# First graph layer: the halves of the features are transposed by the DMA queue into two buffers, and their products with weights come one tile later

## What is computed

```python
output = jnp.matmul(adj / adj_scaling_factor, support_q / support_delta)
...
h = jnp.maximum(_layernorm(x, axis=-1), 0.0)
x = x + _L0_gnn_ref(h, adj, ...)
h = jnp.maximum(_layernorm(x, axis=-1), 0.0)
x = x + _L1_gnn_ref(h, adj, ...)
...
# in _L1_gnn_ref, X = h
for s in range(STEPS):
    A = _adj_from_feats(Xa, W1, W2, W3)   # Q = Xa @ W1, K = Xa @ W3, logits = Q @ W2 @ K.T, top-p softmax
    Xf = R @ Xf
    Xa = A @ Xa
    Z = Z + (Xf @ U1s[s] + Xa @ U2s[s])
```

## Time and profile before

| | |
|---|---|
| median of three runs | 1202.13 us (1200.91 to 1208.22) |
| profiled execution, its time | 1202.94 us |
| profiled execution, its span | 1201.2 us |
| busy, share of the span | PE 91%, DVE 82%, ACT 40%, POOL 24% |
| first layer's tiles 1 to 15 | about 90 to 301 us |
| DMA in the whole span | 171.68 MB, mean 143 GB/s |
| instructions of PE | 5402 |

### The profile page before, as it was taken

The page is one execution under the profiler, slowest core; times in us unless marked ns, Lnnn a source line. Parts: engine busy times, 40 slices in busy tenths (PEclk is TensorE's granted clock), DMA queues, the critical chain, the costliest instruction groups (busy, mean ns, idle before and its releaser), DMA issues.

```text
span 1201.2 us, 16645 instructions
## 1 busy us (share of the span) xinstructions
PE 1097.6 (91%) x5402; PEld 513.7 (43%) x5402; DVE 989.4 (82%) x2144; ACT 483.9 (40%) x920; POOL 286.8 (24%) x255
## 2 busy tenths in 40 slices
PE   0478999999899969999999998989899999999987
PEld 0234454455434434444444444434344444444433
DVE  7877777776389999889999800889999999999997
ACT  1764444443743213453532223874003364351061
POOL 6124333333132311211121210131111111112143
PEclk9898999999999989999999998999899999999999
DMA  7054565553243453163164084023667467576667
GB/s 263 26 192 163 182 211 192 201 200 144 73 141 109 147 131 80 45 149 71 45 151 93 22 175 140 36 80 122 223 208 166 92 186 140 176 195 151 236 143 217
DMA packets 190708, 171.68 MB, mean 143 GB/s; under 512 B 144736, under 2 KB 144736, under 8 KB 186528
## 3 DMA queue, kind: packets, MB, share of 16 engines
q1 hardware_dynamic: 190624, 170.71, 49.5%
HBM read 87.84 MB, written 49.28 MB: 114 GB/s over the span
## 4 chain that ended last, share of the span: by engine, by line
DVE 32%; PE 30%; issue 18%; POOL 7%; ACT 6%; DMA 5%; SPq 1%; POOLq 1%; DVEq 0%; ACTq 0%
PE AB L987 5%; PE RB L987 5%; DVE WS L1605 4%; DVE cand L1837 4%; PE UB L816 4%; DVE WS L1834 3%; PE XB L816 3%; PE AB L989 3%; DVE E L1850 3%; PE RB L989 2%; DMA turns<-E 2%; DVE rows L1685 2%; DVE WS L1842 2%; DVE E L1572 2%; DMA AD<-xu_d 2%
## 5 line engine op out<-in xcount | busy, mean ns | idle before, releaser
L1685 DVE TENSOR_REDUCE rows<-E 128x1 f32<-128x2048 f32 x32 | 73.0, 2281 | 86.0 <-ACT E L1221 85.8
L682 POOL TENSOR_TENSOR RT<-RT,AD 128x512 f32<-128x512 f32 x32 | 55.7, 1739 | 256.9 <-ACT RT L1281 256.8
L1605 DVE SCALAR_TENSOR_TENSOR WS<-E,rows 128x2048 bf16<-128x2048 f32 x43 | 110.6, 2613 | 0.4
L1837 DVE MAX8 cand<-WS 128x8 f32<-128x128 f32 x512 | 102.1, 278 | 1.1
L1842 DVE SCALAR_TENSOR_TENSOR WS<-E,rows 128x2048 f32<-128x2048 f32 x32 | 79.4, 2482 | 0.8
L696 POOL TENSOR_TENSOR XX<-WF,XX 128x512 f16<-128x512 f32 x16 | 26.4, 1651 | 222.8 <-ACT XX L1306 222.8
L1850 DVE SCALAR_TENSOR_TENSOR E<-WS,E 128x2048 f16<-128x2048 f32 x32 | 77.1, 2410 | 2.2 <-issue 1.1
L1834 DVE SCALAR_TENSOR_TENSOR WS<-E,rows 128x2048 f32<-128x2048 f32 x32 | 77.3, 2415 | 1.1
L987 PE MATMUL RB<-XR,turns 128*128 128x512 f16 x256 | 62.1, 387 | 11.3 <-DMA turns<-E 11.3
L1258 ACT ACTIVATE E<-E,nmx 128x2048 f32<-128x2048 f32 x32 | 63.7, 1992 | 5.7 <-DVE nmx L1686 5.7
L987 PE MATMUL AB<-VR,turns 128*128 128x512 f16 x256 | 61.4, 383 | 4.6 <-DMA turns<-E 4.6
(11 more groups left out here) (343 smaller groups left out, 2194.5 us busy)
## 6 DMA issues: line engine op xcount, KB each, us to landing
turns<-adj_parts SPq DMA_DIRECT2D x48, 512.0 KB, 4.0
E<-adjT SPq DMA_DIRECT2D x16, 1024.0 KB, 7.6
adj_parts<-turns SPq DMA_DIRECT2D x16, 1024.0 KB, 5.2
AH<-adj_parts SPq DMA_DIRECT2D x16, 512.0 KB, 4.3
z_d<-UO SPq DMA_DIRECT2D x28, 256.0 KB, 2.3
XR<-x SPq DMA_DIRECT2D x4, 1024.0 KB, 11.8
WS<-U SPq DMA_DIRECT2D x4, 1024.0 KB, 5.3
x_d<-WF SPq DMA_DIRECT2D x16, 256.0 KB, 2.1
```

Source lines behind the costliest of these rows:

```text
L1605: return v.scalar_tensor_tensor(junk[t % 2], e, g4[:, k, t:t + 1], e, op, ALU.mult, accum_out=g4[:, F_, t:t + 1])
L1685: ct(v.tensor_reduce(row(A2)[:, t:t + 1], E[:, slot, :], AX.X, ALU.max))
L1837: i = v.max(cand[:, t, 8 * c:8 * c + 8], WS[:, c * PART:(c + 1) * PART])
```

## The change

The transposes and ScalarE's copy are taken out. SP issues a DMA transpose `x0_turn(t)` from XR to one of two buffers, XT and a part of E that is free in this stage. TensorE's products of a tile come one tile later than before, behind layer t those of tile t-2, and so do the readers of them on ScalarE and GpSimd and the store of UO. The last two tiles' products stand behind the last layer product. Counts of a few semaphores follow (`s_xT`, `s_xTc` start at the second layer now).

```diff
+        x0_turned = (XT, E[:, 7, 0:2 * KC * P // 2].bitcast(F16).rearrange("p (h k c) -> p h k c", h=2, k=KC))
...
+            def x0_turn(t):
+                sp.wait_ge(s_xh, t + 1)
+                sp.wait_ge(s_xl, t + 1 + OPEN)
+                if t < 2:
+                    sp.wait_ge(s_mm1, T + OPEN)
+                else:
+                    sp.wait_ge(s_pk, t - 1)
+                sp.dma_start_transpose(x0_turned[t % 2].rearrange("p h k c -> p (h k) c"),
+                                       XR[:, t, :, :].rearrange("p h d -> p (h d)")).then_inc(s_x0T[t % 2], 16)
...
                 l0_stores(t)
+                x0_turn(t)
                 at_out(t + 1, odd)
-                adj_in(t + 3)
+                if t + 3 < T:
+                    adj_in(t + 3)
                 diag_out(t)
-                post0_stores(t - 1)
+                if t >= 2:
+                    post0_stores(t - 2)
...
             l0_stores(0)
+            x0_turn(0)
             at_out(1, 1)
             adj_in(3)
             diag_out(0)
             u_in(3)
-            for t in range(1, T - 3):
+            for t in range(1, T - 1):
                 l0_tile(t, (t + 1) % 2)
-            for t in range(T - 3, T - 1):
-                l0_stores(t)
-                at_out(t + 1, (t + 1) % 2)
-                diag_out(t)
-                post0_stores(t - 1)
...
+            x0_turn(T - 1)
+            post0_stores(T - 3)
...
+            def l0_tile(t):
+                l0_head(t)
+                v_lo(t - 2, of(VR, t - 2))
+                pk_lo(t - 2, 0, t - 2, s_vl, t - 1)
...
+            l0_head(1)
+            l0_tile(2)
             u_lo(3)
-            with pool.Fori(2, T) as t:
+            with pool.Fori(3, T) as t:
                 l0_tile(t)
+            v_lo(T - 2, of(VR, T - 2))
+            pk_lo(T - 2, 0, T - 2, s_vl, T - 1)
...
                 for j in range(T):
-                    if j == T // 4 and n is not None:
-                        x_halves_turned(n)
...
-            def x_halves_turned(n):
-
-                pe.wait_ge(s_pkc, n + OPEN)
-                pe.wait_ge(s_xh, n + 1)
-                pe.wait_ge(s_xl, n + 1 + OPEN)
-                for h in range(2):
-                    for k in range(KC):
-                        c = h * KC + k
-                        i = tr(XB[:, :].bitcast(F16)[:, c * P:(c + 1) * P],
-                               XR[:, bass.ds(n, 1), h, k * P:(k + 1) * P].rearrange("p o d -> p (o d)"), ident[:, :])
-                i.then_inc(s_xT, 1)
...
+            def post0(n, odd, last=False):
+
+                halves = halves_of_turned(x0_turned[odd])
+                pe.wait_ge(s_x0T[odd], 8 * n - 8 * odd + 16)
+                if last:
+                    pe.wait_ge(s_pkc, n + OPEN)
+                    pk_product(n, XB, halves)
                 pe.wait_ge(s_ue, n + OPEN)
...
+                three(UB[:, :], *halves, lambda k: U10p[:, k, 0, :], lambda k: U10p[:, k, 1, :]).then_inc(s_u, 1)
...
+                three(RB[:, :], *halves, lambda k: U11p[:, k, 0, :], lambda k: U11p[:, k, 1, :]).then_inc(s_v, 1)
+                if not last:
+                    pe.wait_ge(s_wpk, 4)
+                    pe.wait_ge(s_pkc, n + OPEN)
+                    pk_product(n, XB, halves)
...
+            layer0(1, 1)
...
-            with pe.Fori(1, T - 1, 2) as odd:
-                layer0(odd, 1)
-                layer0(odd + 1, 0)
-            layer0(T - 1, 1)
-            x_halves_turned(T - 1)
-            post0_last(T - 1)
+            with pe.Fori(2, T, 2) as even:
+                layer0(even, 0)
+                post0(even - 2, 0)
+                layer0(even + 1, 1)
+                post0(even - 1, 1)
+            post0(T - 2, 0)
+            post0(T - 1, 1, True)
...
-            def xT_halves(n):
-                act.wait_ge(s_xT, n + 1 + OPEN)
-                a(XT[:, :, :, :].rearrange("p h k c -> p (h k c)"), XB[:, :].bitcast(F16), ACT.Copy).then_inc(s_xTc, 1)
-
...
-                if not last:
-                    x_hi(t + 1)
+                if x is not None:
+                    x_hi(x)
...
-            def l0_tile(t):
+            def l0_head(t):
                 turn_free(t + 1)
                 adj_hi(t + 1)
-                xT_halves(t - 1)
-                post0(t - 1)
...
             x_hi(0)
-            l0_tile(1)
+            l0_head(1)
+            x_hi(1)
+            l0_head(2)
+            post0(0, 2)
             u_hi(3)
-            with act.Fori(2, T - 1) as t:
-                l0_tile(t)
-            xT_halves(T - 2)
+            with act.Fori(3, T - 1) as t:
+                l0_head(t)
+                post0(t - 2, t)
+            post0(T - 3, T - 1)
             post0(T - 2)
-            xT_halves(T - 1)
-            post0(T - 1, True)
+            post0(T - 1, last=True)
```

More of the change, by code:

```diff
@@ L243, in build @@
         s_part = sem("s_part")
+        s_x0T = [sem(f"s_x0T{odd}") for odd in range(2)]
         s_sqd = sem("s_sqd")
@@ L848, in x_turned @@
                 if n - T > POSTPONED:
-                    pe.wait_ge(s_xTc, n)
+                    pe.wait_ge(s_xTc, n - T)
                 pe.wait_ge(s_xf, n + 1)
@@ L855, in x_rest, with halves_of_turned, pk_product @@
                 less(XB, x_turned_of(n)[:, 0, :, :].rearrange("p k c -> p (k c)"), minus).then_inc(s_xTs, 1)
+            def halves_of_turned(u):
+                return [lambda k, h=h: u[:, h, k, :] for h in range(2)]
             def halves_turned(n):
-                return [lambda k, h=h: x_turned_of(n)[:, h, k, :] for h in range(2)]
-            def pk_product(n, bank):
-                hi, lo = halves_turned(n)
+                return halves_of_turned(x_turned_of(n))
+            def pk_product(n, bank, halves=None):
+                hi, lo = halves or halves_turned(n)
                 three(bank[:, 0:P], lambda k: WPK[:, k, 0, :], lambda k: WPK[:, k, 1, :], hi, lo).then_inc(s_pk, 1)
-            def post0(n):
-                pe.wait_ge(s_xTc, n + 1)
+            def post0(n, odd, last=False):
[4 more added lines that the diff above has]
+                    pk_product(n, XB, halves)
                 pe.wait_ge(s_ue, n + OPEN)
-                three(UB[:, :], xh, xl, lambda k: U10p[:, k, 0, :], lambda k: U10p[:, k, 1, :]).then_inc(s_u, 1)
+                three(UB[:, :], *halves, lambda k: U10p[:, k, 0, :], lambda k: U10p[:, k, 1, :]).then_inc(s_u, 1)
                 pe.wait_ge(s_ve, n + OPEN)
-                three(RB[:, :], xh, xl, lambda k: U11p[:, k, 0, :], lambda k: U11p[:, k, 1, :]).then_inc(s_v, 1)
-                pe.wait_ge(s_wpk, 4)
-                pk_product(n, XB)
-            def post0_last(n):
-                pe.wait_ge(s_xTc, n + 1)
-                pk_product(n, XB)
-                pe.wait_ge(s_ue, n + OPEN)
-                three(UB[:, :], xh, xl, lambda k: U10p[:, k, 0, :], lambda k: U10p[:, k, 1, :]).then_inc(s_u, 1)
-                pe.wait_ge(s_ve, n + OPEN)
-                three(RB[:, :], xh, xl, lambda k: U11p[:, k, 0, :], lambda k: U11p[:, k, 1, :]).then_inc(s_v, 1)
+                three(RB[:, :], *halves, lambda k: U11p[:, k, 0, :], lambda k: U11p[:, k, 1, :]).then_inc(s_v, 1)
[3 more added lines that the diff above has]
+                    pk_product(n, XB, halves)
             pe.wait_ge(s_sup, NG)
@@ L886, in _, with layer0 @@
             adj_product_lo(0, 0)
+            def layer0(t, h):
+                adj_product_hi(t, h)
+                adj_product_lo(t, h)
+            layer0(1, 1)
             pe.wait_ge(s_upart_h, 2)
             pe.wait_ge(s_upart_l, 2)
-            def layer0(t, h):
-                adj_product_hi(t, h)
-                adj_product_lo(t, h, t - 1)
-                post0(t - 1)
-            with pe.Fori(1, T - 1, 2) as odd:
-                layer0(odd, 1)
-                layer0(odd + 1, 0)
-            layer0(T - 1, 1)
-            x_halves_turned(T - 1)
-            post0_last(T - 1)
+            with pe.Fori(2, T, 2) as even:
[5 more added lines that the diff above has]
+            post0(T - 1, 1, True)
             def logits_chunk(s, gq, t, c):
@@ L999, in u_product @@
                 mm(UB[:, :], id_sw[:, :], XR[:, t, 1, :], start=False, stop=False)
[L1000 removed]
+                pe.wait_ge(s_xTc, t + 1)
                 hi, lo = halves_turned(n)
@@ L1013, in p_and_k @@
                     pe.wait_ge(s_pkc, t + T + OPEN)
-                    pe.wait_ge(s_xTc, t + T + 1)
+                    pe.wait_ge(s_xTc, t + 1)
                 pk_product(t + T, UB)
@@ L1090, in postponed @@
                 pe.wait_ge(s_pkc, 2 * T + OPEN)
-                pe.wait_ge(s_xTc, 2 * T)
+                pe.wait_ge(s_xTc, T)
                 for t in range(POSTPONED, T):
@@ L1178, in v_hi, with post0 @@
                 a(VR[:, bass.ds(t, 1), 0, :].rearrange("p o d -> p (o d)"), RT[:, :], ACT.Copy).then_inc(s_vh, 1)
-            def post0(t, last=False):
+            def post0(t, x=None, last=False):
                 if last:
```

14 lines of the change are left out of this document (4 added, 10 removed).

## The result

The changed kernel takes 1258.49 us (median of 4 runs, 1257.89 to 1259.97) against 1204.86 us before (median of 4, 1200.91 to 1208.22): ratio 1.0448, 95% interval 1.0407 to 1.0489. The profiled execution of after took 1258.02 us with a span of 1256.2, 55.0 more than before.

What follows compares the result with a forecast made beforehand. The prediction took the DMA queue's chain to the diagonal store's landing, 14.00 us a tile, as the bound. Its terms 7.4 + 38 + 0.1 - 2.5 + 7.0 gave +50 us, a median of 1252.5 us, range 1240 to 1269.

Steps and rivals of the forecast that it cites:

- second chain: First-layer tile: ScalarE's casts and adj_lo, about 13.5 us, shorter than the queue's 14.00 by about 0.5 us.
- What the removal is worth: TensorE loses 1.0 us of transposes a tile: nothing counted in the loop, -2.5 us from XF(14) to XF(15).
- The stall on SP: First-layer loop: the transpose waits for x_lo and delays at_out and diag_out; a tile grows from 14.00 to 17.8 us.
- middle stage: Tiles 3 to 13 of the first layer: ten tiles, each growing from 14.00 to 17.8 us, +38 us.
- 0 more, my value: First-layer loop: the transpose's data time lies wholly under SP's issue and adds nothing to a tile.
- The second rival: First-layer loop: the transpose's data time comes on top, 12 x 1.3 = 16 us more, 1268 us; chance 0.17.
- low bound: First-layer loop: queue neighbours further apart, the landing may shrink by 0.6 us a tile; with no clock loss 1243.5 us.
- The start: First layer up to XF(3): later diagonal stores and a displaced u_hi(3) put XF(3) at 142.9 instead of 135.52, +7.4 us.
- The tail: XF(15) to first logits product: UO(13)'s store lands late, two tiles of products open, lowered clock; 18.1 us, +7.0.
- The first: First-layer loop: the stall on SP is covered, needing a landing within 3.7 us; about 1200 us, chance 0.05.
- The third: First-layer loop: the diagonal's landing shrinks half-way, to 5.5 us; 12 x -2 = -24, 1228 us; chance 0.08.
- The clock loss: TensorE at half clock behind gaps: 1.7 us each, costing nothing in the loop and 1.7 us in the tail.

Runs made afterwards that it cites:

- e1: Changed kernel with SP issuing the DMA transpose behind the diagonal store instead of ahead of the adjacency store; 1206.76 us, ratio 1.0034 to the kernel before.
- e5: Kernel before with the 64 KB diagonal store issued ahead of the two 1 MB transfers; 1200.73 us in one run.
- e6: Changed kernel with diagonal store first, transpose last and the second layer's loads late; 1200.66 us, ratio 0.9981 to the kernel before.
- e2: Changed kernel without the DMA transposes' transfer, SP's wait kept; only its first layer is read, 16.33 us a tile (whole 7601.62 us, computing with meaningless numbers).
- e4: Changed kernel with the store of UO for tile 13 put ahead of the last transpose at SP's end; 1258.50 us in one run.
- e10: e6 with ScalarE's cast of the next adjacency tile put between v_hi and pk; 1188.68 us, ratio 0.9881 to the kernel before.
- e9: e1 with the second layer's loads behind the stores of UO(13) and UO(14), and UO(13)'s store ahead of the last transpose; 1207.08 us in one run.
- e7: e6 with ScalarE's cast of the next adjacency tile put directly behind x_hi; 1197.92 us, ratio 0.9944 to the kernel before.

## Why the prediction was right

**What bounds the kernel.** Right: e1 and e5 show it from two sides. The queue's order alone moves the tile between 18.28 and 14.09, and the diagonal store's place alone between 14.00 and 13.69. The second chain was put at 13.5 us and takes 13.69.

**What the removal is worth.** Right: nothing in the loop (before and e1 differ by 0.09 us a tile, e5 and e6 not at all), and 3.2 us at the last layer tile, where 2.5 were expected: TensorE began layer 15 3.14 us ahead of XF(14), 0.6 earlier than forecast.

**The stall on SP.** The mechanism was right in each step: x_lo, then the transpose, at_out, diag_out, landing, 5.30 us to XF. The issues came at +2.68, +4.05 and +5.14 where +2.65, +4.0 and +4.95 were forecast. The size was off in two terms, each by 0.2 us: diag_out goes at +5.14 for +4.95, and it lands 7.80 us later for 7.58. This makes 18.24 instead of 17.8 us, with the means 18.28, and ten tiles make the 4.8 us by which the middle stage, and nearly the whole sum, is short. The prediction had put the transpose's data at "0 more, my value" beside a landing of 7.58. The landing grew by 0.22 us over that of before, the difference of two effects: with the wait alone it is 0.21 shorter (e2), and the transfer adds 0.43 to that. The second rival, which put all 1.3 us on top, had the right sign and a third of the effect; the low bound's 0.6 us less was three times too large.

**The start.** +6.67 for +7.4: XF(2) came at 122.79 for 123.4, since diag_out(1) landed after 7.10 us instead of 7.58, and the displaced u_hi cost what was counted. The prediction's own terms for XF(3) add up to 142.7 and not 142.9, and 50 us on the median of 1202.13 are 1252.1 and not 1252.5; neither slip matters.

**The tail.** +7.65 for +7.0, for the reason that was given: ScalarE waits until the store of UO(13) has landed, and that is set by the 1.5 MB ahead of it. UO(14) came 8.47 us after XF(15) for 7.5 (the loads were to go out 0.7 us ahead of XF(15) and went out with it), so the products of tile 15 began at 11.57 for 10.5; at full clock they take 5.85 for 5.9, and the clock cost 1.3 for 1.7. e4's narrower theory, that the issue behind the transpose counts, is the one that fell. What the prediction did not see is that its wait was worth only 2.47 us: the two tiles of products in a row hold the tail at 14.95 without it.

**The whole.** The median is 6.0 us above the 1252.5, inside the range. Of this 4.4 us are missing in the sum of the stages, mostly the loop; the other stages were off by at most 0.7 us each, the start too long and the tail too short, and these two cancel.

**The rivals.** The first (the stall is covered) is out: the diagonal landed after 7.8 us, not under 3.7. The third (the landing shrinks to 5.5) is out by the same number; the second is answered above.

**What was not foreseen.** ScalarE waits 97.9 us in all for the store of UO, which SP issues behind diag_out and which now lands late (229.1 in the tile that starts with XF at 216). It costs nothing in the loop, since x_hi, the next in ScalarE's program, waits for XF 4.8 us longer anyway; the largest wait in the list is one of no worth. The clock loss was forecast for every gap and for 1.7 us, from one row of before that the earlier trace rows does not show:

```profile
112.42 4.45 PE L816 MATMUL UB<-E,XX 128*128 128x512 f16 x12 [2.81 <-ACT XX L1155]
```

It was there behind all but one of the 13 gaps ahead of hi products in after, with 1.3 to 2.8 us more for the sixteen products (next section). It cost nothing in the loop, as forecast, and 1.3 us in the tail.

## What to carry to other kernels

A DMA issue that has to wait for data is more than one transfer added to the queue: it is a barrier in the program of the engine that issues it. Before putting one in, list what stands behind it, and look for the small transfer among that which somebody waits for; put the waiting one last and the small one first. And an engine relieved of work pays only when no other chain is as long: here three had to be shortened together (queue, casts, TensorE) before removing 1 us of transposes from a tile gave 1 us (e5 to e10, 13.69 to 12.74).

## What the runs showed of the hardware

- A DMA transpose of 256 KB held SP's program for 1.26 us as the tile's first large issue (after) and mostly for 2.4 to 2.6 us behind at_out, adj_in and diag_out (e1). In e6 and e10, behind the same three with diag_out first, it held it for 1.5 to 2.1 us; why less was not tested. The plain transfer issued right behind it took 0.52 instead of 0.34 to 0.37 us for its issue. A 64 KB store behind it landed 0.43 us later than in e2, where it was left out (means of ten tiles).
- What a gap costs TensorE can't be read from its length. In after the sixteen hi products took 5.30 us behind a gap of 2.78 us, 6.38 behind one of 3.76 us, but 3.61 behind one of 3.72 us:

```profile
157.03 5.30 PE L818 MATMUL AB<-E,turns 128*128 128x512 f16 x16 [2.78 <-DVE E L1564]
...
175.53 6.38 PE L818 MATMUL AB<-E,turns 128*128 128x512 f16 x16 [3.76 <-DVE E L1564]
...
230.71 3.61 PE L818 MATMUL AB<-E,turns 128*128 128x512 f16 x16 [3.72 <-DVE E L1564]
```

  Windows of after (stretch, us, busy us of PE, PEld, DVE, ACT, POOL, granted clock, DMA share, GB/s) show 1.00 behind that one and 0.50, which is 1.2 GHz, behind a gap of 5.19 us:

```profile
230.70:234.20 3.50, 3.49 (x17) 1.60 (x18) 2.63 (x6) 0.00 (x0) 1.78 (x2) 1.00 0.00 0
...
248.90:252.50 3.60, 3.55 (x9) 1.34 (x10) 2.73 (x6) 0.00 (x0) 1.78 (x2) 0.50 0.00 0
```

  The prediction's 1.7 us behind each gap lies in the middle of what was found: against 3.62 us at full pace the loss in after is 1.3 to 2.8 us behind twelve gaps and nothing behind one. Behind the gaps of 0.63 to 1.21 us in e1 the groups kept 3.61 us. The tails of before and e5 differ in the same way behind equal gaps (1.00 and 0.58), and so do e9 and e10: behind 1.98 us the U products of tile 15 took 2.6 us at 1.00 and 4.4 at about 0.60.
- GpSimd and VectorE can slow each other, and not always both. In e7 v_lo took 3.15 instead of 1.16 us beside adj_lo, while adj_lo kept its 2.27 us; the short operation of VectorE that overlapped the rest of v_lo took 1.24 instead of 0.28 us. In the kernel before adj_lo took 4.37 us instead of 2.29 beside GpSimd's subtraction over 2048 columns.
